# Row maxima of the first attention item computed in the projection stage, and half of the second item's beside its neighbour's scores

## What is computed

```python
x = _layernorm(x + _L0_attn_ref(x, ...))   # 1 x 2048 x 512, 16 heads of 32
x = _layernorm(x + _L0_ffn_ref(x, ...))    # 8 experts, 2 of them per token, and a shared one
x = _layernorm(x + _L1_attn_ref(x, ...))   # heads of 128
x = _layernorm(x + _L1_ffn_ref(x, ...))

def _L0_attn_ref(x, Wq_sem, Wk_sem, Wq_geo, Wk_geo, Wv, Wo):
    q_geo = _rope(_split_heads(x @ Wq_geo.T, H))   # the like for k; the sem halves are not turned
    v = _split_heads(x @ Wv.T, H)
    q = jnp.concatenate([q_sem, q_geo], axis=-1)
    k = jnp.concatenate([k_sem, k_geo], axis=-1)
    scores = jnp.einsum('bhqd,bhkd->bhqk', q, k) * scale
    scores = jnp.where(causal, scores, jnp.finfo(jnp.float32).min)
    attn = jax.nn.softmax(scores, axis=-1)
    out = jnp.einsum('bhqk,bhkd->bhqd', attn, v)
    return out.transpose(0, 2, 1, 3).reshape(B, S, ATTN_DIM) @ Wo.T
```

## Time and profile before

| | us |
|---|---|
| median of 3 runs | 2221.56 (2220.63 to 2225.43) |
| the profiled execution | 2230.52 |
| its span, first to last instruction | 2228.70 |
| TensorE busy in the span | 2130.8 (96%) |
| VectorE, ScalarE, GpSimd busy | 1190.0, 736.7, 824.5 |
| mean granted clock of TensorE | 0.982 of full speed |

### The profile page before, as it was taken

The page is one execution under the profiler, slowest core; times in us unless marked ns, Lnnn a source line. Parts: engine busy times, 40 slices in busy tenths (PEclk is TensorE's granted clock), DMA queues, the critical chain, the costliest instruction groups (busy, mean ns, idle before and its releaser), DMA issues. The chain is left out here.

```text
span 2228.7 us, 27156 instructions
## 1 busy us (share of the span) xinstructions
PE 2130.8 (96%) x9788; PEld 1456.9 (65%) x9788; DVE 1190.0 (53%) x2306; ACT 736.7 (33%) x1264; POOL 824.5 (37%) x527
## 2 busy tenths in 40 slices
PE   7999999999997999999989999999999999999997
PEld 6875444444442654444467878888877888888886
DVE  5787777777762653222256633223246545564666
ACT  3324555555555322111144422111123211221123
POOL 4354889988999114432222340000003011212100
PEclk9988999999999999999999999999999999999999
DMA  5578355343310626555444360000101010100001
GB/s 180 182 199 191 93 125 139 96 96 72 72 32 18 252 101 230 131 99 92 79 146 141 133 217 29 19 19 29 38 1 57 1 38 20 38 19 28 10 19 57
DMA packets 104604, 197.24 MB, mean 89 GB/s; under 512 B 10384, under 2 KB 27664, under 8 KB 103056
## 3 DMA queue, kind: packets, MB, share of 16 engines
q1 hardware_dynamic: 92064, 162.78, 24.9%
q0 software_dynamic: 11408, 29.69, 5.9%
q10 hardware_dynamic: 1008, 3.15, 0.4%
HBM read 123.82 MB, written 71.75 MB: 88 GB/s over the span
## 5 line engine op out<-in xcount | busy, mean ns | idle before, releaser
L752 ACT ACTIVATE a_probs<-a_stb 128x512 f32<-128x512 f32 (+1 forms) x449 | 241.6, 587 | 189.8 <-PE a_stb L898 93.6
L2306 POOL CAST m_wh<-wst 128x1024 fp32r<-128x1024 f32 x24 | 26.6, 1108 | 719.4 <-POOLq L1591 369.2
L711 POOL TENSOR_TENSOR a_probs<-a_probs 128x1024 f32<-128x1024 f32 (+3 forms) x138 | 266.9, 1960 | 51.2 <-PE a_avb L914 35.7
L789 DVE TENSOR_REDUCE a_mparts<-a_sbank 128x1 f32<-128x512 f32 x384 | 240.4, 683 | 71.8 <-PE a_sbank L866 71.2
L57 PE MATMUL m_gu<-hi,m_wh 128*128 128x512 f32 x512 | 199.8, 390 | 3.0 <-DVE m_h L2436 1.6
L59 PE MATMUL m_gu<-hi,m_wl 128*128 128x512 f32 x512 | 199.4, 389 | 0.0
L58 PE MATMUL m_gu<-lo,m_wh 128*128 128x512 f32 x512 | 199.3, 389 | 0.0
L2385 DVE TENSOR_TENSOR m_h<-m_sg,m_gu 128x512 f32<-128x512 f32 x63 | 43.3, 687 | 191.6 <-ACT m_sg L2336 191.3
L794 DVE CUSTOM_DVE_ANT_0 a_junk<-a_sbank,hidden 128x128 bf16<-128x128 f32 (+3 forms) x256 | 113.7, 488 | 48.8 <-PE a_sbank L866 47.4
L866 PE MATMUL a_sbank<-hi,q 96*128 96x512 f32 (+3 forms) x320 | 121.5, 405 | 7.9 <-DVE a_mparts L789 3.2
L2336 ACT ACTIVATE m_sg<-m_gu 128x512 f32<-128x512 f32 x64 | 38.3, 598 | 261.3 <-PE m_gu L59 261.2
(11 more groups left out here) (324 smaller groups left out, 4943.9 us busy)
## 6 DMA issues: line engine op xcount, KB each, us to landing
hi<-qk SPq DMA_DIRECT2D x66, 256.0 KB, 5.2
qk<-v_hl SPq DMA_DIRECT2D x32, 512.0 KB, 2.9
lo<-qk SPq DMA_DIRECT2D x54, 256.0 KB, 5.2
wst<-in_w_mlp SPq DMA_DIRECT2D x24, 512.0 KB, 3.5
q<-qk SPq DMA_DIRECT2D x42, 256.0 KB, 6.4
xs<-a_zeros POOLq DMA_DIRECT2D x39, 264.0 KB, 3.0
X<-xs SPq DMA_DIRECT2D x39, 264.0 KB, 2.7
v<-vhl SPq DMA_DIRECT2D x16, 512.0 KB, 4.0
```

The lines of the kernel that those rows point to most:

```text
L711: nc.gpsimd.tensor_tensor(probs[to % PSLOTS][:, hs, w0:], probs[to % PSLOTS][:, hs, w0:], probs[other % PSLOTS][:, hs, w0:], ALU.add)\
L752: nc.scalar.activation(to, got, ACT.Exp, scale=SCALE0).then_inc(s["exp_ok"], 1)
L789: nc.vector.reduce_max(to, sbank[:, b, :], AX).then_inc(s["unit_max"], 1)
```

## The change

The 16 units of item 0 move into the first stage. Each stands on TensorE behind a quarter (three matmuls) of a value tile of the last chunk, in the banks of the query-key groups, and VectorE takes their maxima around its last rotation steps. VectorE joins the maxima, TensorE turns them, ScalarE copies them, and ScalarE itself issues their store. At the head of the attention ScalarE waits for that store and issues the read of the row. The early keys are read two stores sooner, behind a wait for the group whose weights they overwrite, and ScalarE's last "high" comes behind the copy of the second value tile.

In the attention, units 0 to 7 of item 1 come ahead of the first scores, its units 8 to 15 go into the first four gaps, two each, and its turn into the fifth. Units of later items are spread from the fifth gap on. SyncE no longer waits for all stores at the head, but for those of the chunks that its next read needs; ScalarE waits for all stores ahead of the exponentials of steps 0 and 1. Items 3 and 4 are both read after the turn of item 1; item 0 has no `max_in` any more. The last lines of the list adapt counters of semaphores.

```diff
-            return [("qk", c, j) for j in range(NG)] + [("v", c, t) for t in range(TC)]
+            return [("qk", c, j) for j in range(NG)] + [("v", c, t) for t in range(TC)] + [("turn", 0, 0)]
...
+                    if c == NC - 1 and j == 1:
+                        sp.wait_ge(s["qk_ok"], k + 1)
+                        for n in range(EARLY):
+                            for dst, src in keys_in(qk_dram, n, 0, kst[n]):
+                                sp.dma_start(dst, src).then_inc(s[f"early{n}"], 16)
...
-                    if c == NC - 1 and j == 1:
-                        for n in range(EARLY):
-                            for dst, src in keys_in(qk_dram, n, 0, kst[n]):
-                                sp.dma_start(dst, src).then_inc(s[f"early{n}"], 16)
...
-            acts = []
+            acts, last_qk = [], ("qk", NC - 1, NG - 1)
             for i, ev in enumerate(events):
                 acts.append(ev)
-                if i > 0 and events[i - 1][0] == "qk":
+                if i > 0 and events[i - 1][0] == "qk" and events[i - 1] != last_qk:
                     acts.append(("high", *events[i - 1][1:]))
+                elif ev == ("v", NC - 1, 1):
+                    acts.append(("high", *last_qk[1:]))
             for what, c, j in acts:
...
+                elif what == "turn":
+                    act.wait_ge(s["turned"], 1)
+                    nc.scalar.activation(msb[:], qk[0:TC * GH, 0, 0, 0:P], ACT.Copy).then_inc(s["mcopy"], 1)
+                    act.wait_ge(s["mcopy"], 1)
+                    act.dma_start(m_dram[0], f32(msb[:])).then_inc(first_max, 16)
...
-            steps.append(("low", NC - 1, NG - 1))
+            at = steps.index(("sum", NC - 1, NG - 1))
+            steps[at:] = [("unit", 0, 0), steps[at], ("unit", 0, 1), ("low", NC - 1, NG - 1), ("unit", 0, 2), ("unit", 0, 3)]
             for what, c, j in steps:
                 k = c * NG + j
+                if what == "unit":
+                    if j == 0:
+                        dve.wait_ge(s["consts"], 48)
+                    w = (j + 1) * P
+                    for u in range(j * GH, (j + 1) * GH):
+                        dve.wait_ge(s["unit_ok"], u + 1)
+                        if u >= 2:
+                            dve.wait_ge(s["unit_max"], u - 1)
+                        nc.vector.tensor_tensor_reduce(
+                            out=junk[:, u % 2, 0:w], in0=qk[:, u // 2 % 2, u % 2, 0:w], in1=hidden[:, CH - w:CH], scale=1.0,
+                            scalar=BIG, op0=ALU.add, op1=ALU.max, accum_out=mparts[:, u % GH * TC + j:u % GH * TC + j + 1])\
+                            .then_inc(s["unit_max"], 1)
...
+                    if j == TC - 1:
+                        dve.wait_ge(s["unit_max"], TC * GH)
+                        nc.vector.tensor_reduce(nm[:], mparts[:].unsqueeze(2), AX, ALU.max, negate=True).then_inc(s["nm_ok"], 1)
...
+            def unit(t, h):
+                u = t * GH + h
+                if u == 0:
+                    pe.wait_ge(s["early0"], 16 * 6)
+                    pe.wait_ge(s["consts"], 48)
+                if u < 4:
+                    pe.wait_ge(s["qkf_ok"], NC * NG - 1 + u // 2)
+                else:
+                    pe.wait_ge(s["unit_max"], u - 3)
+                w = (t + 1) * P
+                nc.tensor.matmul(qk[:, u // 2 % 2, u % 2, 0:w], qst[0:96, 0, h, t * P:(t + 1) * P], kst[0][0:96, h, 0:w],
+                                 start=True, stop=True).then_inc(s["unit_ok"], 1)
...
-                    last.then_inc(s["v_ok"], 1)
+                        if d == ND - 1:
+                            last.then_inc(s["v_ok"], 1)
+                        if c == NC - 1:
+                            unit(j, d)
+                elif what == "turn":
+                    pe.wait_ge(s["nm_ok"], 1)
+                    nc.tensor.transpose(qk[0:TC * GH, 0, 0, 0:P], nm[:], ident[:]).then_inc(s["turned"], 1)
...
-    here, have = 0.0, corners[early[-1]][1]
+    here, have = gaps[4][0], corners[early[-1]][1]
...
+        if n == EARLY:
+            at_gap = 4
         for j, unit in enumerate(units[n]):
             amount += cost(n, unit)
+            if n == 0:
+                continue
             if n in early:
-                before.append(("unit", n, j))
+                (before if j < 8 else in_gap[(j - 8) // 2]).append(("unit", n, j))
...
-                before.insert(len(before) - len(units[n]) + 4, ("turn", n - 1))
-            if n == early[-1]:
-                before.append(("turn", n))
+                in_gap[4].append(("turn", n))
...
-                sp.wait_ge(s["mcopy"], n + 1)
+                sp.wait_ge(s["mcopy"], n)
...
-                sp.wait_ge(s["mstore"], 16 * (n + 1))
+                sp.wait_ge(s["mstore"], 16 * n)
...
-            for store in stored:
-                sp.wait_ge(store, 16 * NC * NG // 2)
-            work, queries = [], -1
+            work, queries, sure = [], -1, 0
...
-                soon = order.index(("turn", n - EARLY - 1)) if n > EARLY else -1
+                soon = order.index(("turn", max(1, n - EARLY - 1))) if n > EARLY else -1
...
-                work.append((order.index(("turn", n)), len(work), "m", n, 0, 0))
+                if n > 0:
+                    work.append((order.index(("turn", n)), len(work), "m", n, 0, 0))
             for _, _, what, n, j, after in sorted(work):
+                chunks = 1 + {"q": items[n][0], "k": j, "m": -1}[what]
+                if chunks > sure:
+                    sure = chunks
+                    for store in stored:
+                        sp.wait_ge(store, 16 * chunks * NG // 2)
...
+            act.wait_ge(first_max, 16)
+            act.dma_start(f32(qs[0][96:97]).rearrange("o h n -> o (h n)"),
+                          m_dram[0].rearrange("r q -> (r q)").unsqueeze(0)).then_inc(mrow[0], 16)
...
+                    if i < 2 and h == per - 1:
+                        for store in stored[i::2]:
+                            act.wait_ge(store, 16 * NC * NG // 2)
```

More of the change, by code:

```diff
@@ L158, with layer0_qkv @@
 SWAP = [(r + 8 if r < 24 else r - 8) if r >= HD0 // 2 else r for r in range(HD0)]
-def layer0_qkv(nc, xT, w_qk, w_v, rope, masks, eye, X, V, hi, lo, qst, consts, qk_dram):
+def layer0_qkv(nc, xT, w_qk, w_v, rope, masks, eye, X, V, hi, lo, qst, consts, qk_dram, m_dram):
     with ExitStack() as ctx:
@@ L172, in layer0_qkv @@
         rotated = m.sb("rotated", [P, 2, CH])
+        junk = m.sb("junk", [P, 2, CH], BF16)
+        mparts = m.sb("mparts", [P, TC * GH])
+        nm = m.sb("nm", [P, TC * GH])
+        msb = m.sb("msb", [TC * GH, P], F32R)
         xh, xl = (a[:, 0:2, :].rearrange("p b (d n) -> p b d n", d=ND) for a in (hi, lo))
@@ L181, in layer0_qkv @@
         names = ("wa w0 w1 w2 xd0 xd1 xd2 xd3 x0 x1 cs0 cs1 xhi xlo whi_a wlo_d whi_p wlo_p qk_ok qkf_ok v_ok vs_ok rot_ok "
-                 "t1_ok sin_ok sum_ok hi_ok lo_ok clear_ok hstore0 hstore1 lstore0 lstore1 consts early0 early1").split()
+                 "t1_ok sin_ok sum_ok hi_ok lo_ok clear_ok hstore0 hstore1 lstore0 lstore1 consts early0 early1 "
+                 "unit_ok unit_max nm_ok turned mcopy").split()
         s = {k: m.sem(k) for k in names}
+        first_max = m.sem("first_max")
         wload, xload, csload = [s[f"w{i}"] for i in range(3)], (s["x0"], s["x1"]), (s["cs0"], s["cs1"])
@@ L577, in attention0_plan, with layer0_attention @@
     return items, steps, first, final, units, loads, last_use, order
-def layer0_attention(nc, stage_before, stored, landed, qx, qk_dram, m_dram, xs_dram, acc_dram, token, V, X, hi, lo, fifth, qst, consts, early, out_w, first_o):
+def layer0_attention(nc, stage_before, stored, landed, first_max, qx, qk_dram, m_dram, xs_dram, acc_dram, token, V, X, hi, lo, fifth, qst, consts, early, out_w, first_o):
     items, steps, first, final, units, loads, last_use, order = attention0_plan()
@@ L591, in layer0_attention @@
     slot_of = {load: at for at, load in enumerate(loads)}
-    last_unit = {n: max(k for ev, k in unit_no.items() if ev[1] == n) for n in range(len(items))}
+    last_unit = {n: max(k for ev, k in unit_no.items() if ev[1] == n) for n in range(1, len(items))}
     NI = len(items)
@@ L754, in _ @@
                     n = ev[1]
-                    act.wait_ge(s["turned"], n + 1)
-                    if n >= 2:
-                        act.wait_ge(s["mstore"], 16 * (n - 1))
+                    act.wait_ge(s["turned"], n)
+                    if n >= 3:
+                        act.wait_ge(s["mstore"], 16 * (n - 2))
                     nc.scalar.activation(msb[:, n % 2, :], sbank[0:GH * TC, ring[ev] % 3, 0:P], ACT.Copy)\
@@ L798, in _ @@
                         dve.wait_ge(s["unit_max"], k + 1)
-                        if n >= 2:
-                            dve.wait_ge(s["turned"], n - 1)
+                        if n >= 3:
+                            dve.wait_ge(s["turned"], n - 2)
```

(10 more changed lines are left out.)

2 lines of the change are left out of this document (1 added, 1 removed).

## The result

The changed kernel takes 2234.22 us in the median of 16 runs (2229.77 to 2244.94), the kernel before 2224.74 in 16 runs beside them (2220.63 to 2233.43). The ratio over these runs is 1.0034, with a 95% interval from 1.0021 to 1.0047: slower by 7.6 us (4.7 to 10.5), where 1.0 us was forecast. The two medians themselves stand 9.5 us apart, which lies within that interval. The forecast time of 2222.6 us, with a range from 2217 to 2231, was added to a median of 3 runs, 2221.56; the 16 runs put the kernel before 3.2 us higher. So of the 11.6 us between 2222.6 and 2234.22, 3.2 belong to the base and 8.4 to the change. The profiled execution took 2231.46 us for a span of 2229.6, only 0.9 us more than that of before.

A forecast was written before the change was run, and what follows sets the result against it. TensorE, busy 96% of the span, was taken as the bound. First scores at 166.8 plus 17.4, 0.5, 15.9 and 15.9 gave 216.5 against 215.50; this 1.0 us added to the 2221.56 median made 2222.6 us, range 2217 to 2231.

The forecast's parts named there:

- the low clock in the values: Rival: clock stays 0.50 through the last chunk's values and units, some 10 us more, 2232.6 us; chance 0.13.
- the row behind the reads: Rival: item 0's row of maxima waits behind SyncE's six reads, scores 4 to 6 us later, about 2228; chance 0.05.
- Item 1 then takes 13.14 + 7 x 0.39 = 15.9: Attention, item 1: seven more units among its scores at 0.39 us each lengthen it from 13.14 to 15.9 us.
- From there on both kernels run one order of work: From item 3's first scores on, what is won or lost by then (1.0 us late) is carried to the end.
- The stop: First stage, last chunk: TensorE waits 5.5 us for item 0's keys before the first unit; bounds 4 to 7.
- The 2.4 us charged for that: Work lost in the values and units to a 0.50 clock behind TensorE's wait for item 0's keys: 2.4 us.
- the keys in time: Rival: item 0's keys land before 139.4, or the wait is short without low clock; up to 7.9 us faster, 2214.7; chance 0.10.
- Values, units, turn, seam: End of first stage: values 10.2 us, units 3.9, then turn and seam; attention starts at 163.9, 11.2 us later.
- The row of maxima: Ahead of item 0's scores: store lands in 1.5 us, read takes 1.6; scores at 166.8, 2.3 us early.
- The covers: GpSimd's first sum is ready 1.1 us before the denominators; SyncE's read of item 2's row is level with its scores.
- the queue becomes the bound: Rival: slower reads or item 1's late turn make item 2 wait for its row, 3 us, 2225.6; chance 0.15.
- The bounds: Forecast's own bounds: stop 4 to 7, clock -2.4 to +2, store +1.5, queue +1, giving 2219 to 2227 us.

The follow-up runs named there:

- 10: The changed kernel with at most two units behind a score in item 1 alone; ratio to the kernel before 1.0035.
- 13: The changed kernel with the turn of item 2 moved three scores later, behind the sixth score of item 1; ratio to the kernel before 1.0041.
- 9: The kernel before with only item 0's units and maxima moved into the first stage, and eight units in item 1 drawn together behind two scores; ratio 1.0046.
- 14: 9 with the turn of item 2 placed between the two groups of four units; ratio to the kernel before 1.0033.
- 6: The changed kernel with overwritten filler matmuls in TensorE's stop, ahead of item 0's turn, behind early units and ahead of the first scores; ratio to before 1.0032.
- 7: 5 with overwritten filler matmuls added on TensorE up to the first scores; ratio to the kernel before 1.0006.
- 8: The changed kernel with item 0's keys read sooner, at most two units in each of the first 64 gaps, and filler matmuls; ratio to before 1.0008.
- 5: The kernel before with only item 0's units and maxima moved into the first stage, and item 0's keys read sooner; ratio 1.0001.

## Why the prediction was wrong

The account of the first 30 us held. The sign held too, but by luck as much as by reason: the sum was only 1.0 us, and the likeliest outcome (0.64) was a time within 0.2% of before. The time is 0.34% longer, to which 0.25 was given, most of it for two rivals that did not come, the low clock in the values and the row behind the reads. The step that failed is **"Item 1 then takes 13.14 + 7 x 0.39 = 15.9"**. It priced seven units more at full clock, and item 1 lost that clock. The scores of item 4 come 6.35 us late (95.64 against 89.29) where 1.0 was forecast. The miss of 5.3 comes apart so:

- *The clock in item 1, 2.7 us.* 19.17 against 16.47 for the same 23 units without 0.50 (10), whose order differs a little. Within one program, 13's, it is 18.39 with 6.8 us of 0.50 against 16.09 without, 2.3 us; so 2.3 to 2.7 belong to the clock. The forecast weighed the low clock at the stop and as a rival in the values, and never asked where the second part makes TensorE wait for VectorE again. The trace of before had the pattern: units at VectorE's pace from 152.7 to 161.0, and a granted clock of 0.59 in that stretch.
- *The price of a unit, 1.0 us.* At full clock seven units made item 1 longer by 16.47 - 13.14 = 3.33, 0.48 each, and two made item 2 longer by 1.22, 0.61 each; 0.39 was taken, out of one item's difference, a mean in which waits for banks in denser gaps don't show; that these waits are the difference is argued, not shown.
- *The eighth unit, 0.6 us.* "From there on both kernels run one order of work" was off by one unit: eight are moved, seven fall into items 0 to 2, the eighth into item 3, which takes 12.95 instead of 12.32.
- *Seam and item 0, 1.0 us.* First scores 0.5 later than forecast, item 0 0.5 longer.

Of the other steps:

- *The stop*: 5.5 us forecast, 6.2 measured, with the keys' landing as releaser: the last of them landed at 133.00 + 11.0 = 144.0, 3.7 us behind the store ahead of them (131.21 + 9.1 = 140.3), where 3.6 was taken. The clock behind it was 0.50, and came back. The 2.4 us charged for that came from no row; 0.50 lasted 3.8 us from the first unit on (144.00 to 147.8), at half speed some 1.9 us of lost work (an estimate). Right, and the rivals of the keys in time and of the values at the low clock both fell.
- *Values, units, turn, seam*: 11.2 us later forecast, 10.5 measured. Right.
- *The row of maxima*: the store landed in 1.4 us (1.5 forecast). The read was taken at 1.6 us, from a stretch without SyncE's reads; from its issue at 162.00 to the scores at 165.53 it was 3.5. The transfers of that stretch in the changed kernel (queue, count, KB, us to landing):

```profile
q<-qk SPq DMA_DIRECT2D x3, 256.0 KB, 4.8
lo<-qk SPq DMA_DIRECT2D x3, 256.0 KB, 7.0
```

  SyncE's six reads, issued from 161.51 on, took 4.8 and 7.0 us in the median of three, and the row came before most of them. The rule of the Trainium skill, DMA: Bandwidth & Descriptors (Queues, rings and completion order), that an engine takes turns between queues, agrees with that: the row didn't stand behind them. But it shared the engines with them, at some 1.9 us if the whole difference is put down to that.
- *The covers*: they held. The two first sums of GpSimd end ahead of the denominators, and the row of item 2 is read 6.2 us ahead of the scores at 203.09, which wait for nothing. The forecast had them closer: 1.1 us and level. (Its 183.4 for the denominators is not the 166.8 + 16.9 = 183.7 of its own words; nothing hangs on that.)

```profile
177.37 3.61 POOL L767 TENSOR_TENSOR a_probs<-a_probs 128x768 f32<-128x768 f32 x2 [1.17 <-PE a_avb L976]
...
182.50 1.04 PE L992 MATMUL a_den<-a_probs,a_ones 128*32 128x512 f32 x8
...
196.88 0.23 SPq L703 DMA_DIRECT2D q<-max  x1
```

  The rival in which the queue becomes the bound fell. The change became slower by a mechanism that none of the rivals named.
- *The bounds*: stop, clock, store and queue add up to -3.9 and +6, so 2218.7 to 2228.6, where 2219 to 2227 is written. No term stood for a lower clock in items 1 and 2.

Taken as a whole, the change shifts work instead of removing it: the seam comes 10.5 us later for first scores 1.8 us sooner, and what the second part takes out of the gap ahead of the scores it puts back between them, at 0.5 to 0.6 us a unit and with a clock that falls.

## What to carry to other kernels

Where a change moves work at another engine's pace into a dense stretch of TensorE, look for the waits that it makes there, and price the stretch at both clocks; a mean per unit out of a stretch without such waits is too low. Count moved instructions to the last one, past the point where the sum ends. And profile a kernel more than once before a clock stretch is put down to its order: one execution can be without it by chance.

## What the runs showed of the hardware

- *The clock can fall in one execution of a program and not in the next.* Each of two programs had 0.50 in item 1 in one execution of three, that of 13 with nearly the same busy time ahead of it (3.92 us at 1.00, 4.04 ahead of the fall, of 4.50). The Trainium skill, TensorE: Matmul & The Clock Gate (What's actually happening), says that the same kernel differs from run to run in how many matmuls run cold at its start; these profiles show the like in the middle of a kernel. The same page (A second HAM failure mode: psum-queue depth-cycling) tells of a kernel whose clock swings because TensorE pauses often while it goes round its banks; the waits of the bunch, 0.28 and 0.41 us, are of that kind, but the runs agree only in part: 9 and 14 draw units together as well and kept 1.00 in item 1.
- *Fillers move the low clock, they don't remove it.* In 6 it was gone from 138 to 169.8 and came from 169.8 to 180.0, behind a wait of 1.29 us in front of item 1's turn. In 7 and 8 it came inside item 0 for 10.2 us.
- *The part that nobody touched varies more than the effect.* From item 5's scores to the end of the span the profiles took 1968.1 (10) to 1979.3 us (5), 1972.8 before and 1969.1 after, with stretches of 0.50 at places that differ between executions (294 and 437 us in the profile of before, neither in that after). This, and the last query-key matmul that came 1.8 us sooner, is why two profiles' spans can stand 0.9 us apart where the kernels stand 7.6 apart: 6.4 - 1.8 - 3.7 = 0.9.
